# Expert stage of a graph and mixture-of-experts kernel: who issues the weight loads, and who copies the turned rows

## Chip, core and metric

The kernel runs on one core of one Trainium2 chip. The metric is the device time of one execution in microseconds (us), lower is better. The core has TensorE (PE in the views), VectorE (DVE), ScalarE (ACT), GpSimd (POOL) and SyncE (SP), each with its own stream of instructions that is carried out in order, and 16 DMA engines that they share. "SPq" or "ACTq" in a row is an instruction of that engine's queue that issues a DMA or waits.

## The reference, cut to what matters

The program is two graph layers and two mixture-of-experts layers on 10,000 rows of 512 numbers. The change touches only the last part of the second mixture layer: each row is sent to two of 64 experts, and each expert is a small net of two layers, 512 to 32 and 32 to 512, with a gelu between.

```python
se = sel.reshape(-1)                                   # 2 experts for each of the rows
pos = jnp.take_along_axis(jnp.cumsum(oh, axis=0) - 1, se[:, None], axis=1)[:, 0]
keep = pos < C
buf = jnp.zeros((E, C, d), x.dtype).at[se, posc].add(xr)
h = jax.nn.gelu(jnp.einsum('ecd,edf->ecf', buf, W1), approximate=False)   # W1: 64 x 512 x 32
y = jnp.einsum('ecf,efd->ecd', h, W2)                                     # W2: 64 x 32 x 512
out = y[se, posc] * keep[:, None].astype(x.dtype)
```

## The kernel before, in words

The kernel is a row of stages that follow each other with a barrier between; all but one stay as they are. The stage of the change ("the expert stage") computes `h` and `y` for the rows in the order of their experts. The 20,000 row copies, each expert's share rounded up to whole tiles of 128 rows, make 219 tiles (`LISTED`); a tile has one expert, and which one is read at run time from a small table `trow`. Tiles are worked in groups of four (`tiles(g)`, `NG` = 55 groups, the last has three). For a tile `t` of group `g`:

- **gather**: POOL fetches the tile's 128 rows with an indirect DMA into `xg`, a ring of eight tiles; it waits for the turn of tile `t - 8`.
- **weights**: SP reads the expert's number from `trow` (`value_load`) and issues two DMAs of 64 KB, the first layer's weights into `we1` and the second layer's into `we2`. Both are rings of `WR` = 6 groups, and both are counted on one semaphore per ring place, `p_w`. Before it starts a group, SP waits until the group six earlier is through its second layer (`p_dn`).
- **turn**: PE transposes the 128 x 512 tile in four matmuls into a PSUM bank; there are two banks for this, so it waits for the copy of tile `t - 2` (`p_T`).
- **copy**: ACT copies the turned tile from PSUM to `gT` (L2081).
- **up**: PE multiplies the four tiles of the group by `we1` (L2049), 16 matmuls in the program, each recorded as two.
- **gelu**: ACT writes `hg` from the result (L2089).
- **down**: PE multiplies `hg` by `we2`, one matmul for each tile into four PSUM banks (L2060), each recorded as two.
- **result**: DVE copies each of them from PSUM to `yo` (L2118), a ring of three groups; it waits for the store of the group three earlier (`p_st`).
- **store**: ACT issues one DMA of 1 MB from `yo` to memory for the group (L2094).

In round `g` of its loop PE does turns 1 and 2 of group `g`, `up(g - 1)`, turns 3 and 4 of `g`, `down(g - 2)`. ACT does two copies, `gelu(g - 1)`, two copies, `store(g - 3)`. The order on every engine is written out by hand, and nothing is reordered. The two waits on which PE's rounds hang are

```python
pe.wait_ge(p_T, tiles(g)[-1] + 1)       # up(g): the four turned tiles are copied
pe.wait_ge(p_w[g % WR], 32 * sum(len(tiles(k)) for k in range(g % WR, g + 1, WR)))  # both weights are there
```

Of the kernel before, what the change touches and what calls it, by code (L numbers as in the profile page):

```python
# [14 lines left out]
P = 128  # L15
# [47 lines left out]
def gnn_ffn(nc, x, xTt, src, dst, Wl, Wr, att, gbias, Wc0, b1c, W2e, b2e, WT, bG, hashp, M1, M2, out):  # L63
    ctx = ExitStack()
    with ctx:
# [1933 lines left out]
        we2 = sb("we2", [P, WR, D], F32, pt)  # L1999
        hg = sb("hg", [P, 2, P], F32, pt)  # L2000
        yo = sb("yo", [P, 12, D], F32, pt)
        p_ld, p_w, p_st = sems("p_ld", 8), sems("p_w", WR), sems("p_st", 3)
        p_0, p_tr, p_T, p_up, p_h, p_dn, p_y = (sem("p_" + n) for n in "0 tr T up h dn y".split())
        NG = -(-LISTED // 4)

# [4 lines left out]
        with nc.Block() as block:  # L2010
            @block.sync
            def _(sp):
                for g in range(NG):
                    if g >= WR:
                        sp.wait_ge(p_dn, tiles(g - WR)[-1] + 1)
                    for t in tiles(g):
                        e = sp.value_load(trow[0:1, t + 2 * P:t + 2 * P + 1], min_val=0, max_val=ME - 1)
                        j = t % 4
                        sp.dma_start(we1[:, g % WR, j, :], M1[bass.ds(e * P, P), :]).then_inc(p_w[g % WR], 16)
                        sp.dma_start(we2[MF * j:MF * (j + 1), g % WR, :], M2[bass.ds(e * MF, MF), :])\  # L2020
                            .then_inc(p_w[g % WR], 16)

            @block.gpsimd
            def _(pool):
# [9 lines left out]
            def _(pe):  # L2034
# [5 lines left out]

                def up(g):
                    pe.wait_ge(p_T, tiles(g)[-1] + 1)
                    pe.wait_ge(p_w[g % WR], 32 * sum(len(tiles(k)) for k in range(g % WR, g + 1, WR)))
                    if g >= 2:
                        pe.wait_ge(p_h, g - 1)
                    for k in range(DK):
# [6 lines left out]

                def down(g):
                    pe.wait_ge(p_h, g + 1)
                    for t in tiles(g):
                        j = t % 4
                        if g >= 1:
                            pe.wait_ge(p_y, t - 3)
                        nc.tensor.matmul(bank[4 + j], hg[MF * j:MF * (j + 1), g % 2, :],  # L2060
                                         we2[MF * j:MF * (j + 1), g % WR, :], start=True, stop=True).then_inc(p_dn, 1)
# [12 lines left out]

            @block.scalar
            def _(act):
                def copy(t):
                    act.wait_ge(p_tr, t + 1)
                    if t >= 8:
                        act.wait_ge(p_up, (t - 8) // 4 + 1)  # L2080
                    act.activation(gT[:, t % 8, :, :].rearrange("p k n -> p (k n)"), bank[t % 2], ACT.Copy)\  # L2081
                        .then_inc(p_T, 1)

                def gelu(g):
                    act.wait_ge(p_up, g + 1)
# [5 lines left out]
                def store(g):  # L2091
# [2 lines left out]
                    act.dma_start(YL[4 * g * P:(4 * g + n) * P, :].rearrange("(t p) c -> p t c", p=P),  # L2094
                                  yo[:, 4 * (g % 3):4 * (g % 3) + n, :]).then_inc(p_st[g % 3], 16)

                for g in range(NG + 3):
                    if g < NG:
                        for t in tiles(g)[:2]:
                            copy(t)  # L2100
                    if 1 <= g <= NG:
                        gelu(g - 1)
                    if g < NG:
                        for t in tiles(g)[2:]:
                            copy(t)
                    if g >= 3:
                        store(g - 3)
                for k in range(3):
                    act.wait_ge(p_st[k], 16 * len(range(k, NG, 3)))

            @block.vector
            def _(dve):
                for t in range(LISTED):
                    g = t // 4
                    if t % 4 == 0 and g >= 3:
                        dve.wait_ge(p_st[g % 3], 16 * (g // 3))
                    dve.wait_ge(p_dn, t + 1)
                    nc.vector.tensor_copy(yo[:, t % 12, :], bank[4 + t % 4]).then_inc(p_y, 1)  # L2118
        end_phase(pt)


# [135 lines left out]
```

## Time and profile before

| what | value |
|---|---|
| median of 3 runs | 3016.11 us (3004.85 to 3016.43) |
| the profiled execution, its own time | 3008.54 us |
| its span, first to last instruction | 3006.8 us |
| granted clock of TensorE, mean | 0.873 |
| first weight DMA issued / last result copied | 2282.9 us / 2753 us of the span |

The span is one execution; the time outside it is 1.74 us. A view that names a window counts from the start of the span. Busy time of an engine leaves out register, branch, semaphore and DMA-issuing instructions, so SP, which only issues, never shows as busy: how it spends its time is read from the starts of its rows. The DMA share is the mean busy share of the 16 DMA engines; as packets overlap it can pass 1.

### The profile page before, as it was taken

Reading aid. Unit: us, or ns where it says so; the run is one execution under the profiler, and the core shown is the slowest. Engines: PE = TensorE matmul, PEld = TensorE weight load, DVE = VectorE, ACT = ScalarE, POOL = GpSimd, SP = SyncE. Lnnn points to the kernel's source line nnn. Section 1 sums busy time; section 2 is a strip of 40 time slices with the busy share of each in tenths; the row PEclk is TensorE's granted clock in tenths of the full one; section 3 lists DMA queues with packets and bytes.
Section 4 is the critical chain, followed back from the end, with each engine's and each line's share of the span. In section 5 each row is a group of like instructions: output and inputs, shape, how many; then the busy total and the mean of one; then the engine's idle time right before and its main releaser. Section 6 shows DMA issues by size and latency. Waiting matters only on the chain. (4 is left out here: it accounts for less than half of the span.)

```text
span 3006.8 us, 43565 instructions
## 1 busy us (share of the span) xinstructions
PE 2155.7 (72%) x11422; PEld 1277.3 (42%) x11422; DVE 1674.5 (56%) x5206; ACT 1079.5 (36%) x2314; POOL 1992.6 (66%) x2711
## 2 busy tenths in 40 slices
PE   8999999677776577787867499999954656664000
PEld 3444444355554355455522156666632434442000
DVE  5666665455554787788711157777762222234665
ACT  0000000055553577777833245555532322231000
POOL 3677776677773688888866436777765444451776
PEclk9999999889998799999979799999976777786555
DMA  6999999389995666666489666676625888875999
GB/s 206 140 157 145 153 145 162 120 257 311 312 314 181 202 196 209 209 198 204 172 319 397 256 229 209 213 213 211 207 78 169 289 285 275 284 259 180 332 378 345
DMA packets 358165, 685.64 MB, mean 228 GB/s; under 512 B 54603, under 2 KB 88387, under 8 KB 357921
## 3 DMA queue, kind: packets, MB, share of 16 engines
q1 hardware_dynamic: 243096, 401.02, 47.5%
q0 software_dynamic: 80496, 218.00, 22.7%
q10 hardware_dynamic: 34329, 63.84, 6.2%
q8 instruction: 95, 1.56, 0.2%
q14 instruction: 149, 1.22, 0.1%
HBM read 433.75 MB, written 266.57 MB: 233 GB/s over the span
## 5 line engine op out<-in xcount | busy, mean ns | idle before, releaser
L2030 POOL DMA_INDIRECT xg<-n_rows,ids x219 | 218.4, 997 | 223.0 <-PE psum L155 177.9
L2118 DVE COPY yo<-psum 128x512 f32<-128x512 f32 x219 | 136.0, 684 | 335.7 <-PE psum L2060 335.7
L149 PE MATMUL psum<-wl,xT 128*128 128x512 f32 x632 | 288.8, 600 | 3.9 <-DVE xr L507 3.9
L149 PE MATMUL psum<-wg,yT 128*128 128x512 f32 x632 | 286.4, 596 | 0.0
L149 PE MATMUL psum<-wr,xT 128*128 128x512 f32 x632 | 284.1, 592 | 0.0
L149 PE MATMUL psum<-wc,x1T 128*128 128x264 f32 x632 | 174.7, 424 | 94.6 <-DVE hb L1165 93.5
L2167 POOL DMA_INDIRECT q<-slot_outputs,qs x158 | 171.9, 1088 | 95.7 <-issue 47.9
L1579 POOL DMA_INDIRECT slot_tokens<-sl x158 | 173.1, 1095 | 67.1 <-issue 51.2
L779 ACT ACT_TABLE_LOAD x1 | 1.3, 1283 | 588.4 <-PEq L80 588.4
L2049 PE MATMUL psum<-gT,we 128*32 128x128 f32 x1752 | 79.2, 336 | 164.8 <-issue 159.7
L149 PEld LDWEIGHTS psum<-wr,xT 128*128 128x128 f32 x632 | 120.1, 190 | 151.2 <-issue 151.2
L2081 ACT ACTIVATE gT<-psum 128x512 f32<-128x512 f32 x219 | 122.4, 595 | 166.3 <-PE psum L155 165.8
L149 PEld LDWEIGHTS psum<-wc,x1T 128*128 128x128 f32 x632 | 122.7, 204 | 128.6 <-issue 106.3
L1390 PE MATMUL psum<-gg,sm 128*128 128x512 f32 x236 | 129.0, 687 | 66.9 <-DVE sm L1378 57.1
L149 PEld LDWEIGHTS psum<-wl,xT 128*128 128x128 f32 x632 | 115.1, 190 | 125.9 <-issue 125.9
L149 PEld LDWEIGHTS psum<-wg,yT 128*128 128x128 f32 x632 | 114.7, 192 | 114.7 <-issue 114.7
L1369 POOL DMA_INDIRECT gg<-gcn_rows,idx x118 | 119.7, 1014 | 63.1 <-PE psum L1390 28.2
L650 POOL DMA_INDIRECT gl<-xl_rows,idx x118 | 134.6, 1141 | 39.5 <-issue 30.5
L654 POOL DMA_INDIRECT gr<-xr_rows,idx x118 | 133.7, 1133 | 36.0 <-issue 31.4
L155 PE MATMUL psum<-ident,xg 128*128 128x128 f32 x876 | 145.1, 317 | 16.5 <-DMA xg<-n_rows,ids 16.0
L149 PE MATMUL psum<-hp,x3T 128*128 128x256 f32 x632 | 150.0, 380 | 2.3 <-ACT x3T L1882 2.3
L1248 PE MATMUL psum<-w,hT 128*128 128x512 f32 x316 | 150.7, 600 | 0.0
(318 smaller groups left out, 5523.9 us busy)
## 6 DMA issues: line engine op xcount, KB each, us to landing
slot_outputs<-yo ACTq DMA_DIRECT2D x54, 1024.0 KB
x_rows<-x SPq DMA_DIRECT2D x158, 256.0 KB, 3.2
edge_sums<-eo SPq DMA_DIRECT2D x29, 1056.0 KB, 7.6
edge_sums<-go SPq DMA_DIRECT2D x29, 1024.0 KB
we<-in_M SPq DMA_DIRECT2D x438, 64.0 KB
xT<-in_xTt SPq DMA_DIRECT2D x79, 256.0 KB
xl_rows<-xl SPq DMA_DIRECT2D x79, 256.0 KB
xr_rows<-xr SPq DMA_DIRECT2D x79, 256.0 KB
```

The costliest lines, as they stand in the source:

```text
L149: last = nc.tensor.matmul(ps, lhs[:, k, :], rhs[:, k, :], start=(k == 0), stop=(k == DK - 1))
L155: last = nc.tensor.transpose(ps[:, k * P:(k + 1) * P], rows[:, k * P:(k + 1) * P], ident[:])
L650: pool.indirect_dma_start(gl[:, w % 16, :], None, XL, bass.IndirectOffsetOnAxis(idx[:, 0, w:w + 1], 0), bounds_check=NP - 1, oob_is_err=Fa ...
L654: pool.indirect_dma_start(gr[:, w % 8, :], None, XR, bass.IndirectOffsetOnAxis(idx[:, 1, w:w + 1], 0), bounds_check=NP - 1, oob_is_err=Fal ...
L1248: nc.tensor.matmul(bank[3 + 4 * h], hT[:, h, k, :], w2[:, k, :], start=(k == 0), stop=False)
L1369: pool.indirect_dma_start(gg[:, w % 8, :], None, GR, bass.IndirectOffsetOnAxis(idx[:, 0, w:w + 1], 0), bounds_check=NP - 1, oob_is_err=Fal ...
L1390: nc.tensor.matmul(bank[j], sm2[:, u % 2, j, :], gg[:, w % 8, :], start=True, stop=True)\
L1579: pool.indirect_dma_start(IDXF, bass.IndirectOffsetOnAxis(sl3[:, k, t:t + 1], 0), sl3[:, 2, t:t + 1], None, bounds_check=ME * SLOTS * P - ...
L2030: pool.indirect_dma_start(xg[:, t % 8, :], None, XN3, bass.IndirectOffsetOnAxis(ids[:, t:t + 1], 0), bounds_check=NP - 1, oob_is_err=False ...
L2081: act.activation(gT[:, t % 8, :, :].rearrange("p k n -> p (k n)"), bank[t % 2], ACT.Copy)\
L2118: nc.vector.tensor_copy(yo[:, t % 12, :], bank[4 + t % 4]).then_inc(p_y, 1)
L2167: pool.indirect_dma_start(q0[:, b % 3, t % 4, k, :], None, YL, bass.IndirectOffsetOnAxis(qs[:, b % 3, t % 4, k:k + 1], 0), bounds_check=LI ...
```

## The change

SP issues only the loads of the first layer's weights, and waits for `up` of the group six earlier in place of `down`. ACT issues the loads of the second layer's weights, three groups ahead of the group whose rows it is at, counted on semaphores of their own, `p_v`; `up` waits for `p_w` alone and `down` for `p_v`. The copies of the turned tiles move from ACT to DVE, which does the four copies of group `g` and then the four results of group `g - 2`. No DMA is added or taken away, and the bytes are the same.

```diff
-        p_ld, p_w, p_st = sems("p_ld", 8), sems("p_w", WR), sems("p_st", 3)
+        p_ld, p_w, p_v, p_st = sems("p_ld", 8), sems("p_w", WR), sems("p_v", WR), sems("p_st", 3)
...
             def _(sp):
                 for g in range(NG):
                     if g >= WR:
-                        sp.wait_ge(p_dn, tiles(g - WR)[-1] + 1)
+                        sp.wait_ge(p_up, g - WR + 1)
                     for t in tiles(g):
                         e = sp.value_load(trow[0:1, t + 2 * P:t + 2 * P + 1], min_val=0, max_val=ME - 1)
-                        j = t % 4
-                        sp.dma_start(we1[:, g % WR, j, :], M1[bass.ds(e * P, P), :]).then_inc(p_w[g % WR], 16)
-                        sp.dma_start(we2[MF * j:MF * (j + 1), g % WR, :], M2[bass.ds(e * MF, MF), :])\
-                            .then_inc(p_w[g % WR], 16)
+                        sp.dma_start(we1[:, g % WR, t % 4, :], M1[bass.ds(e * P, P), :]).then_inc(p_w[g % WR], 16)
...
                 def up(g):
-                    pe.wait_ge(p_w[g % WR], 32 * sum(len(tiles(k)) for k in range(g % WR, g + 1, WR)))
+                    pe.wait_ge(p_w[g % WR], 16 * sum(len(tiles(k)) for k in range(g % WR, g + 1, WR)))
...
                 def down(g):
                     pe.wait_ge(p_h, g + 1)
+                    pe.wait_ge(p_v[g % WR], 16 * sum(len(tiles(k)) for k in range(g % WR, g + 1, WR)))
...
             def _(act):
-                def copy(t):
-                    act.wait_ge(p_tr, t + 1)
-                    if t >= 8:
-                        act.wait_ge(p_up, (t - 8) // 4 + 1)
-                    act.activation(gT[:, t % 8, :, :].rearrange("p k n -> p (k n)"), bank[t % 2], ACT.Copy)\
-                        .then_inc(p_T, 1)
+                def weights(g):
+                    if g >= WR:
+                        act.wait_ge(p_dn, tiles(g - WR)[-1] + 1)
+                    for t in tiles(g):
+                        e = act.value_load(trow[0:1, t + 2 * P:t + 2 * P + 1], min_val=0, max_val=ME - 1)
+                        j = t % 4
+                        act.dma_start(we2[MF * j:MF * (j + 1), g % WR, :], M2[bass.ds(e * MF, MF), :])\
+                            .then_inc(p_v[g % WR], 16)
...
+                for g in range(3):
+                    weights(g)
                 for g in range(NG + 3):
-                    if g < NG:
-                        for t in tiles(g)[:2]:
-                            copy(t)
                     if 1 <= g <= NG:
                         gelu(g - 1)
-                    if g < NG:
-                        for t in tiles(g)[2:]:
-                            copy(t)
                     if g >= 3:
                         store(g - 3)
+                    if g + 3 < NG:
+                        weights(g + 3)
...
             def _(dve):
-                for t in range(LISTED):
+                def copy(t):
+                    dve.wait_ge(p_tr, t + 1)
+                    if t >= 8:
+                        dve.wait_ge(p_up, (t - 8) // 4 + 1)
+                    nc.vector.tensor_copy(gT[:, t % 8, :, :].rearrange("p k n -> p (k n)"), bank[t % 2]).then_inc(p_T, 1)
+
+                def result(t):
                     g = t // 4
                     if t % 4 == 0 and g >= 3:
                         dve.wait_ge(p_st[g % 3], 16 * (g // 3))
                     dve.wait_ge(p_dn, t + 1)
                     nc.vector.tensor_copy(yo[:, t % 12, :], bank[4 + t % 4]).then_inc(p_y, 1)
+
+                for g in range(NG + 2):
+                    for t in tiles(g) if g < NG else ():
+                        copy(t)
+                    for t in tiles(g - 2) if g >= 2 else ():
+                        result(t)
```

On SP, one tile in the middle of the stage stood so before (the load of the expert's number, two register instructions, the weights of each layer with a register instruction ahead of each):

```order
L2017 TENSOR_LOAD trow
L2017 ISA x2
L2019 ISA
L2019 DMA we<-in_M 128x128
L2020 ISA
L2020 DMA we<-in_M 32x512
```

The same place after the change:

```order
L2017 TENSOR_LOAD trow
L2017 ISA x2
L2018 ISA
L2018 DMA we<-in_M 128x128
L2017 TENSOR_LOAD trow
```

The second DMA and its register instruction are gone from SP's tile, and the next tile's number follows at once.

On ACT, one round in the middle of the stage stood so before (copies to `gT`, the gelu to `hg`, the store from `yo`; the semaphores have the allocator's names):

```order
L2089 ACTIVATE hg<-psum 128x128 [waits a_xr,a_mm]
L2081 ACTIVATE gT<-psum 128x512 [waits a_mm,a_nm] x2
L2094 DMA slot_outputs<-yo 128x4x512 [waits a_m]
L2081 ACTIVATE gT<-psum 128x512 [waits a_mm,a_nm] x2
L2089 ACTIVATE hg<-psum 128x128 [waits a_xr,a_mm]
```

And now, from the gelu through the store to the first two of the four weight loads that follow it:

```order
L2089 ACTIVATE hg<-psum 128x128 [waits a_nq,a_al]
L2094 DMA slot_outputs<-yo 128x4x512 [waits a_aw]
L2079 TENSOR_LOAD trow [waits a_nq]
L2079 ISA x2
L2081 ISA
L2081 DMA we<-in_M 32x512
L2079 TENSOR_LOAD trow
L2079 ISA x2
L2081 ISA
L2081 DMA we<-in_M 32x512
```

The four copies are gone from ACT's round, and four loads of a number with one DMA each stand behind the store, ahead of the next gelu.

## Rows read from the trace of the kernel before

**Rows 1.** Busy time by stretch of the expert stage.

```profile
...
core 0: us, PE busy (x) PEld busy (x) DVE busy (x) ACT busy (x) POOL busy (x), PEclk, DMA share, GB/s
2283.00:2313.00 30.00, 18.40 (x183) 12.67 (x184) 3.22 (x6) 11.47 (x21) 23.13 (x22) 0.74 0.75 218
2313.00:2743.00 430.00, 264.13 (x2847) 180.08 (x2845) 127.16 (x205) 127.07 (x254) 197.74 (x199) 0.80 0.84 274
2743.00:2758.00 15.00, 6.17 (x38) 2.90 (x38) 5.60 (x10) 0.27 (x1) 0.00 (x0) 0.61 0.59 215
...
```

**Rows 2.** Who waited for whom, 2282 to 2775 us: total, times, longest.

```profile
...
DVE yo L2118 <- PE psum L2060: 335.7, 54, 24.8
...
POOL xg L2030 <- PE psum L155: 177.9, 77, 9.9
PEld psum L2049 <- issue: 171.1, 51, 10.2
...
PEld psum L155 <- DMA xg<-n_rows,ids: 21.6, 14, 9.4
...
PEld psum L2049 <- ACT gT L2081: 5.7, 4, 1.8
...
```

**Rows 3.** Users of the weight tiles up to 2528.2 us: ns min/median/max, first and last start.

```profile
...
L2049 PE MATMUL psum<-gT,we x896: 269/297/423, 2298.0 to 2522.5; 128*32 128x128 f32 x180
...
L2019 SPq DMA_DIRECT2D we<-in_M x116: 337/348/1273, 2282.9 to 2527.2; - x116
...
L2020 SPq DMA_DIRECT2D we<-in_M x116: 331/332/1508, 2283.5 to 2527.7; - x116
...
```

**Rows 4.** Timeline ahead of the `up` at 2533 us.

```profile
...
2523.85 0.37 ACTq L2094 DMA_DIRECT2D slot_outputs<-yo  x1
...
2524.17 1.51 SPq L2020 DMA_DIRECT2D we<-in_M  x1
...
2527.16 0.35 SPq L2019 DMA_DIRECT2D we<-in_M  x1
...
2527.69 0.33 SPq L2020 DMA_DIRECT2D we<-in_M  x1
...
2528.87 0.35 SPq L2019 DMA_DIRECT2D we<-in_M  x1
...
2530.51 0.35 SPq L2019 DMA_DIRECT2D we<-in_M  x1
...
2533.25 1.08 PE L2049 MATMUL psum<-gT,we 128*32 128x128 f32 x16 [7.36 <-issue]
```

**Rows 5.** Both weight DMAs of SP and `up`, whole stage.

```profile
...
L2049 PE MATMUL psum<-gT,we x1752: 269/273/423, 2298.0 to 2746.3; 128*32 128x128 f32 x195
...
L2019 SPq DMA_DIRECT2D we<-in_M x219: 337/348/1273, 2282.9 to 2740.2; - x110
...
L2020 SPq DMA_DIRECT2D we<-in_M x219: 331/332/1749, 2283.5 to 2740.7; - x110
...
```

**Rows 6.** POOL's timeline, gathers that wait for nothing.

```profile
...
2287.53 1.00 POOL L2030 DMA_INDIRECT xg<-n_rows,ids  x1 [0.30 <-issue]
2288.83 1.00 POOL L2030 DMA_INDIRECT xg<-n_rows,ids  x1 [0.31 <-issue]
...
```

**Rows 7.** Costliest groups by form, 2282 to 2775 us.

```profile
...
L2118 DVE COPY yo<-psum 128x512 f32<-128x512 f32 x219 | 136.0, 684 | 335.7 <-PE psum L2060 335.7
L2081 ACT ACTIVATE gT<-psum 128x512 f32<-128x512 f32 x219 | 122.4, 595 | 166.3 <-PE psum L155 165.8 <-issue 0.3
...
L2089 ACT ACTIVATE hg<-psum 128x128 f32<-128x128 f32 x54 | 15.0, 278 | 203.2 <-PE psum L2049 203.2
...
```

**Rows 8.** Timeline of PE, DVE and ACT, a round at either clock.

```profile
...
2500.49 1.14 PE L2060 MATMUL psum<-we,hg 32*128 32x512 f32 x8
...
2501.56 1.09 PE L155 MATMUL psum<-ident,xg 128*128 128x128 f32 x8
...
2501.72 2.48 DVE L2118 COPY yo<-psum 128x512 f32<-128x512 f32 x4 [7.92 <-PE psum L2060]
...
2502.26 1.08 ACT L2081 ACTIVATE gT<-psum 128x512 f32<-128x512 f32 x2 [1.02 <-PE psum L155]
...
2502.59 1.08 PE L2049 MATMUL psum<-gT,we 128*32 128x128 f32 x32
...
2504.62 1.14 PE L2060 MATMUL psum<-we,hg 32*128 32x512 f32 x8
...
2505.69 1.09 PE L155 MATMUL psum<-ident,xg 128*128 128x128 f32 x8
...
2515.01 1.94 PE L2049 MATMUL psum<-gT,we 128*32 128x128 f32 x32 [8.23 <-issue]
...
2516.88 1.97 PE L155 MATMUL psum<-ident,xg 128*128 128x128 f32 x8
...
2518.78 1.96 PE L2060 MATMUL psum<-we,hg 32*128 32x512 f32 x8
...
```

**Rows 9.** DMA queues and issues, 2282 to 2775 us: packets, MB, share.

```profile
...
q10 hardware_dynamic: 28912, 57.41, 33.2%
q0 software_dynamic: 17520, 41.01, 25.5%
q1 hardware_dynamic: 43104, 30.83, 21.9%
...
qx<-x_rows SPq DMA_DIRECT2D x2, 1024.0 KB, 7.8
...
```

**Rows 10.** Windows in which the DMA engines are full.

```profile
...
2315.00:2320.00 5.00, 2.27 (x16) 1.15 (x16) 0.79 (x2) 1.10 (x2) 3.86 (x4) 1.00 1.02 339
2320.00:2325.00 5.00, 3.42 (x42) 2.71 (x41) 1.70 (x3) 1.47 (x3) 4.00 (x4) 0.75 1.05 354
2325.00:2330.00 5.00, 3.17 (x22) 1.86 (x20) 2.48 (x4) 2.28 (x4) 3.08 (x4) 0.91 1.01 342
2330.00:2335.00 5.00, 3.70 (x48) 2.56 (x48) 0.00 (x0) 1.47 (x3) 1.90 (x2) 0.77 1.01 346
...
```

**Rows 11.** The last stage, full too.

```profile
...
2845.00:2920.00 75.00, 0.00 (x0) 0.00 (x0) 50.72 (x81) 0.00 (x0) 58.53 (x55) 0.50 1.01 371
...
```

## The prediction

> **What bounds the kernel now.** I take the stage first. The windows show that it lasts some 470 us and that no engine is busy all the time: in the long middle stretch PE is busy 264 of 430 us, DVE 127, ACT 127, POOL 198, and the DMA share is 0.84 at 274 GB/s [rows 1]. So the stage waits for something that is not busy time. The table of waits names it by exclusion: DVE and POOL wait for PE (335.7 and 177.9 us), and PE in turn waits 171.1 us ahead of `up` for "issue", which is the name for a wait whose releaser the view doesn't know; for gathers it waits 21.6 us, for ACT's copies 5.7 us [rows 2]. `up` waits for copies, for the gelu of two groups before and for the weights, and the weights are the one of these that the view can't name.
>
> Counting confirms it. Up to 2528.2 us SP had issued 116 loads of each kind, which is 29 groups, while PE had 896 records of `up`, 28 groups of 32 [rows 3]. The last DMA of group 29 went out at 2527.69, and its `up` starts at 2533.25 after 7.36 us of idle time [rows 4]. The ring would let SP be six groups ahead; it is never more than one. So SP's stream sets the pace: from the first `up` at 2298.0 to the last, whose records end the row at 2746.3 and which starts some 1.5 us ahead of that, 54 rounds take 446.8 us, **8.27 us a round** [rows 5].
>
> Where does SP's time go? When nothing disturbs it, tile follows tile every 1.64 us (2528.87 to 2530.51 [rows 4]), though its two DMA instructions take only 0.348 and 0.332 us [rows 5]; the rest is reading the number and preparing registers. 219 tiles at 1.64 us are 359 us. From first to last issue it is 457.8 us [rows 5], so 99 us, 1.8 us a round, are extra. They come in bursts behind a store: ACT issues one at 2523.85, and SP's DMA at 2524.17 takes 1.51 us instead of 0.33, the next starts 3.0 us later [rows 4].
>
> **The change, part by part.** I work out the pace that each resource would allow in a round of four tiles; the slowest sets it.
>
> *SP.* A tile loses the step from its first DMA to its second, 0.53 to 0.54 us (2527.16 to 2527.69 [rows 4]): 1.64 − 0.54 = 1.10, 4.4 us a round undisturbed. With all of the extra 1.8 us it is 6.2. The new wait for `up` six groups back stands ahead of loads that are then several groups early; it costs nothing while SP is ahead.
>
> *ACT.* It loses four copies of 0.56 us [rows 7]. It gains four loads, each a number read and one DMA. No row shows ACT doing this; the nearest are SP's, so 1.1 us each, 4.4 in all. With the store's 0.37 [rows 4] and the gelu's 0.28 [rows 7] that is 5.1 us. If ACT takes the extra 1.8 us too, 6.9. Behind the loads on ACT stand the next gelu and store; the gelu is needed by a `down` one round later, so up to a round's delay is covered. The twelve loads ahead of the loop take 13 us; PE's first `up` comes 15 us after SP's first issue [rows 5], so they are covered too, with about 2 us to spare.
>
> *DVE and PE.* DVE gains 219 copies of the form that it already does in 0.684 us [rows 7], four in a row in 2.48 us [rows 8]: eight copies are some 5.0 to 5.5 us. They are chained to PE. At the high clock (2.4 GHz) the first result starts 1.23 us after `down` (2500.49 to 2501.72), four results end 2.5 us later, then the copy of the next group's first tile follows, 0.6 to 0.7 us and 0.3 for the release. Only then can PE do the third turn; two turns (0.55 us each, 1.09 for both [rows 8]) and the next `down` follow. That is 1.23 + 2.5 + 0.9 + 1.1 = **5.75 us** a round. PE's own work is 4.13 us (2501.56 to 2505.69). At the low clock (1.2 GHz) turns take 1.97 a pair, `up` 1.94, `down` 1.96, so PE's work alone is 7.84 us [rows 8].
>
> *POOL.* 1.30 us a gather (2287.53 to 2288.83 [rows 6]), 5.2 us a round.
>
> *DMA.* The three queues moved 57.41 + 41.01 + 30.83 = 129.25 MB, of which 2.1 MB (the two `qx` loads) belong to the next stage [rows 9]: 127.2 MB, 2.31 MB a round. What do the engines give when full? In four windows in a row the share is at or above 1.01 at 339 to 354 GB/s [rows 10], mean 345. That is **6.7 us a round**; at 354 it is 6.5. Now they run at 274 GB/s [rows 1].
>
> The slowest is the DMA, before every engine's stream. The bursts behind the stores fit this: they fall where the engines are full. I take 7.1 us, 6% above the floor, since gathers come in pairs behind the turns and PE falls to the low clock in some waits. Start-up (2283 to 2298) and tail (after the last `up`) stay. The sum: 54 × (8.27 − 7.1) = 63 us off 3008.5 us, the profiled execution's own time, 2945.3. That execution lies 7.6 us under the median and 3.7 above the lowest run; half way between the two, at 3012.3, I start from: **2949 us**, 2.2% less than the median.
>
> Two rules of the Trainium skill bear on this. "DMA: Bandwidth & Descriptors", section "Issuing engines are not separate DMA queues", says that to start DMAs on several engines only saves sequencer time, usually small beside the transfer. By that rule the change would be worth little; the trace shows that here the sequencer's time is what is late. The same page puts HBM for a core at about 358 GB/s, by which a round would be 6.5 us and the time some 13 us less than with 6.7; the last stage shows 371 GB/s [rows 11], so it is not a hard ceiling in this kernel, and with this stage's mix of small loads no window passed 354.
>
> **The rivals.**
>
> *A, the forecast (0.68):* DMA-bound, 6.6 to 7.6 us a round, 36 to 90 us gained.
>
> *B, the extra time behind the stores moves to both queues (0.22).* What lengthens SP's DMA instructions might be not full engines but the generation of the store's descriptors, which both queues share. For it: the delay begins within 0.3 us of the store's issue [rows 4]. Against it: it lasts longer than the store's own 0.37 us. ACT now issues its first load right behind its own store and SP's loads compete too. If ACT gets one and a half times the present extra, a round is 5.1 + 2.7 = 7.8 us, and the gain 25 us: 2987 us on the same scale. At 5.1 + 3.2 nothing is gained. The skill's "Perfetto Trace Analysis", section "DMA Instruction — HWDGE (DVE, Sync)", describes such a shared block with a lock; this trace can't tell it from full engines.
>
> *C, no gain (0.05).* PE stays at the low clock, which alone makes 7.84 us a round, and the waits for gathers bring it above 8. Against it: PE at the low clock with 7.84 of work a round would be busy throughout, and the round that followed a wait of 8.23 us ran at the low clock while one without a wait ran at the high one [rows 8]. Within 15 us of before.
>
> *D, slower (0.05): the copies wait behind the results.* On DVE a result of group `g` waits until the store of group `g − 3` has landed. Before, only results stood behind it; now the turned tiles' copies do, and with them PE. The store has about three rounds less four results to be issued and to land: 3 × 7.1 − 2.5 = 18.8 us. ACT may issue it up to 5 us late. A 1 MB transfer takes 7.8 us from issue to landing in the next stage [rows 9], and 1.04 MB at a third of 345 GB/s would take 9.1 us, so 14 us or less is used. It decides when issue and landing together pass 3 × 8.27 − 2.5 = 22.3 us; then each 3 us more cost 1 us a round. With 27 us a round would be 9.8 us, 83 us slower, 3095 us.
>
> **How the numbers follow.** Three runs of this kernel differ by 0.4%; about 0.5%, 15 us, is what can be told from no change. A lies between 2922 and 2976, B between 2976 and 3004. The bounds of the floor (6.5 at 354 GB/s, gain 96 us) give 2916 at the low end; 7.84 us a round gives a gain of 23 us and 2989 at the high end. The range of **2916 to 2989** leaves out about 2 in 10: part of B, and C and D. Faster by over 0.5% (under 3001): nearly all of A and B, 0.88. Within 0.5%: the rest of B, and C, 0.07. Slower: 0.05.
>
> **What the profile after would show.** Right: the DMA share of the middle stretch at 0.93 or more and 315 to 340 GB/s; the first to last `up` in 365 to 400 us; PE's "issue" wait ahead of `up` gone or under 40 us, since SP is several groups ahead; PE waiting for gathers more than 21.6 us. Copies on DVE at 0.68 us. B would show itself by ACT's DMA and SP's lasting long with a share under 0.9, and by `down` or the gelus late. D: DVE idle ahead of `yo`, and POOL waiting for PE longer than 178 us. I would be wrong if loads cost ACT much more than the 1.1 us of SP, or if the full engines move this mix at under 300 GB/s.

## The result and the profile after

The kernel after takes 2914.15 us (median, 2910.81 to 2920.22 in 4 runs) against 3010.48 us before; the ratio is 0.9677, 95% interval 0.9647 to 0.9707, so it is 3.2% faster. The prediction said 2949 us and a range of 2916 to 2989: right way, but the time lies 2 us below the range. The profiled execution took 2912.88 us against 3008.54, 95.7 us less where 63 was worked out.

The windows of the stretches after, which answer to [rows 1]; the middle stretch is cut where the tiles become empty (columns as there):

```profile
...
core 0: us, PE busy (x) PEld busy (x) DVE busy (x) ACT busy (x) POOL busy (x), PEclk, DMA share, GB/s
2288.00:2318.00 30.00, 19.22 (x176) 12.80 (x176) 13.21 (x20) 2.12 (x4) 23.12 (x22) 0.68 0.89 249
2318.00:2600.00 282.00, 204.56 (x2340) 130.82 (x2336) 207.12 (x333) 11.65 (x42) 167.74 (x169) 0.90 1.05 366
2600.00:2650.00 50.00, 38.98 (x504) 25.38 (x504) 44.22 (x73) 2.22 (x8) 29.89 (x30) 1.00 0.81 263
...
```

The DMA share of the long stretch went from 0.84 at 274 GB/s to 1.05 at 366 GB/s, and DVE's busy time from 30% to 73%. From 2600 us on the share falls to 0.81, since those tiles hold hardly any rows: in that window the gather queue moves 0.26 MB. The DMA view of it (queue: packets, MB, share):

```profile
...
q10 hardware_dynamic: 6236, 11.49, 66.4%
q1 hardware_dynamic: 2822, 1.28, 9.3%
q0 software_dynamic: 2570, 0.26, 4.2%
...
```

The users of the weight tiles, which answer to [rows 5] (ns min/median/max, first and last start):

```profile
...
L2046 PE MATMUL psum<-gT,we x1752: 272/273/423, 2303.8 to 2653.7; 128*32 128x128 f32 x195
...
L2081 ACTq DMA_DIRECT2D we<-in_M x219: 327/328/3992, 2287.8 to 2638.8; - x110
L2018 SPq DMA_DIRECT2D we<-in_M x219: 337/338/1912, 2287.8 to 2625.5; - x110
...
```

First `up` to last `up` took 447 us and takes 349, **6.47 us a round** in place of 8.27. SP ends its loads 27 us ahead of the last `up`, in place of 4. ACT's load instruction reaches 3992 ns: the delays that SP alone had, ACT has now too. The waits in the stage answer to [rows 2]:

```profile
...
PE psum L155 <- DVE gT L2115: 87.7, 50, 4.9
POOL xg L2027 <- PE psum L155: 86.3, 70, 4.8
...
DVE yo L2122 <- DMA slot_outputs<-yo: 43.7, 19, 4.0
...
PEld psum L155 <- DMA xg<-n_rows,ids: 19.9, 14, 9.4
...
PEld psum L2046 <- issue: 9.9, 54, 0.3
...
```

PE's wait ahead of `up` for a releaser that the view can't name fell from 171.1 to 9.9 us. New are 87.7 us in which PE's third turn waits for DVE's copy, and 43.7 us in which DVE waits for a store to land. Two rounds of the last stretch, PE and DVE, which answer to [rows 8]:

```profile
...
2619.84 1.09 PE L155 MATMUL psum<-ident,xg 128*128 128x128 f32 x8
2619.99 2.49 DVE L2122 COPY yo<-psum 128x512 f32<-128x512 f32 x4 [0.42 <-PE psum L2058]
...
2620.86 1.08 PE L2046 MATMUL psum<-gT,we 128*32 128x128 f32 x32
...
2622.39 1.28 DVE L2115 COPY gT<-psum 128x512 f32<-128x512 f32 x2
...
2623.22 1.23 PE L155 MATMUL psum<-ident,xg 128*128 128x128 f32 x8 [1.28 <-DVE gT L2115]
...
2623.89 1.29 DVE L2115 COPY gT<-psum 128x512 f32<-128x512 f32 x2 [0.21 <-PE psum L155]
...
2624.38 1.14 PE L2058 MATMUL psum<-we,hg 32*128 32x512 f32 x8
...
2625.45 1.09 PE L155 MATMUL psum<-ident,xg 128*128 128x128 f32 x8
...
2631.06 1.09 PE L155 MATMUL psum<-ident,xg 128*128 128x128 f32 x8
...
```

The first turn starts at 2619.84, 2625.45 and 2631.06: **5.61 us a round**, the chain that the prediction put at 5.75. In it the third turn waits 1.28 us for the first copy (2623.22), and DVE is busy all but 0.6 us. The stretch before is a mix of such rounds and longer ones: by the starts of `up`, 22 of the first 45 rounds take less than 5.75 us and the others up to 11.7, so their mean of 6.67 us is a pace over many rounds, and not the length of a typical one.

### The profile page after: what moved, and what is told of

The parts are those of the page before. It is cut to its first block and busy times, and to the rows that moved or that the text cites. A ratio compares the mean times of both kernels' runs of the same rounds, so it can differ in the third digit from the quotient of the medians.

```text
span 2911.1 us, 44199 instructions
## 1 busy us (share of the span) xinstructions
PE 2142.8 (74%) x11396; PEld 1260.6 (43%) x11422; DVE 1812.3 (62%) x5425; ACT 957.5 (33%) x2095; POOL 1991.2 (68%) x2711
## 5 line engine op out<-in xcount | busy, mean ns | idle before, releaser
L155 PE MATMUL psum<-ident,xg 128*128 128x128 f32 x876 | 143.2, 304 | 102.6 <-DVE gT L2115 87.7
L155 PEld LDWEIGHTS psum<-ident,xg 128*128 128x128 f32 x876 | 105.7, 154 | 176.7 <-issue 156.8
L2122 DVE COPY yo<-psum 128x512 f32<-128x512 f32 x219 | 135.9, 684 | 65.8 <-DMA slot_outputs<-yo 43.7
L2115 DVE COPY gT<-psum 128x512 f32<-128x512 f32 x219 | 142.1, 685 | 34.0 <-PE psum L155 33.8
L393 POOL DMA_INDIRECT node_rows<-qv,idx x118 | 121.8, 1032 | 46.3 <-issue 41.3
```

What stands on the lines that cost most here:

```text
L155: last = nc.tensor.transpose(ps[:, k * P:(k + 1) * P], rows[:, k * P:(k + 1) * P], ident[:])
L393: pool.indirect_dma_start(NQF, bass.IndirectOffsetOnAxis(idx[:, 2, w:w + 1], 0), qv[:, w:w + 1], None, bounds_check=NP - 1, oob_is_err=False)\
L2115: nc.vector.tensor_copy(gT[:, t % 8, :, :].rearrange("p k n -> p (k n)"), bank[t % 2]).then_inc(p_T, 1)
```

## The experiments

The runs were made on more than one chip, and fell in two groups: in one the kernel before takes 3007 to 3010 us, in the other 3091 to 3104 (called chips of the slower kind). Ratios compare runs of one chip; where times of a stage from two kinds of chip stand beside each other, it is said. What makes the two groups is open: chip number 0 of the record stands in both (3007 and 3098 us). "First to last `up`" is read from the row of the matmuls into `psum` from `gT` and `we`, less the 1 to 1.5 us that the last group's records take.

**Was SP's stream the limit before?** Three edits, all on a chip of the slower kind; on that kind the whole change gives about as much as on the first (3010.41 against 3104.42 us, 3.0%, one execution each). The first keeps the split of the loads but leaves the copies on ACT (against the kernel after):

```diff
             def _(act):
+                def copy(t):
+                    act.wait_ge(p_tr, t + 1)
...
                 for g in range(NG + 3):
+                    if g < NG:
+                        for t in tiles(g)[:2]:
+                            copy(t)
...
             def _(dve):
-                for g in range(NG + 2):
-                    for t in tiles(g) if g < NG else ():
-                        copy(t)
```

> The kernel after, but the copies of the turned tiles stay on ScalarE, two ahead of the gelu and two behind it; VectorE does results only. Theory 1 (before, SyncE's stream of instructions set the pace; the split is what gains): SyncE is several groups ahead of up and its wait is gone. ScalarE's round is then the longest: four copies 2.2 to 2.4 us, gelu 0.28, store 0.37, four loads of about 1.25 us each as in the kernel after, some 8 us, in one stream, so most of the gain is lost: 2975 to 3010 us. Rival (SyncE's stream was not the limit, ScalarE's copies were, and moving them gave the gain): slower than before by the 4 x 1.1 us a round that ScalarE gains, 54 x 4.4 = 240 us at most.

Measured: ratio 0.9956 (0.9937 to 0.9975), 439.5 us from first to last `up`. Its timeline (start, length) shows why:

```profile
...
2602.51 0.28 ACT L2096 ACTIVATE hg<-psum 128x128 f32<-128x128 f32 x1
...
2603.41 0.60 ACT L2079 ACTIVATE gT<-psum 128x512 f32<-128x512 f32 x1 [0.61 <-PE psum L155]
...
2604.26 0.60 ACT L2079 ACTIVATE gT<-psum 128x512 f32<-128x512 f32 x1 [0.26 <-PE psum L155]
2604.27 0.39 ACTq L2101 DMA_DIRECT2D slot_outputs<-yo  x1
2605.39 5.55 ACTq L2088 DMA_DIRECT2D we<-in_M  x4
...
2611.04 1.09 ACT L2079 ACTIVATE gT<-psum 128x512 f32<-128x512 f32 x2 [6.18 <-DMA slot_tokens<-sl]
...
2611.78 0.41 PE L155 MATMUL psum<-ident,xg 128*128 128x128 f32 x2 [3.77 <-ACT gT L2079]
```

ACT issues the four loads from 2605.39 to 2610.94, and only then copies; PE's third turn waits 3.77 us for it. The split alone gives 0.4%.

The second moves the copies to DVE and leaves SP both loads (against the kernel before):

```diff
             def _(act):
-                    if g < NG:
-                        for t in tiles(g)[:2]:
-                            copy(t)
...
             def _(dve):
-                for t in range(LISTED):
+                for g in range(NG + 2):
+                    for t in tiles(g) if g < NG else ():
+                        copy(t)
+                    for t in tiles(g - 2) if g >= 2 else ():
+                        result(t)
```

> The kernel before, but VectorE copies the turned tiles (four copies, then four results, as in the kernel after); SyncE still issues both layers' weights. Theory 1 (SyncE's stream is the limit): the pace stays at 8.3 us a round, within 15 us of before (3000 to 3025), up still waits for weights. Rival (the copies' move gains by itself): 30 us or more faster.

Measured: ratio 1.0006 (0.9986 to 1.0026). The move of the copies alone gives nothing. The third doubles the suspected cost (against the kernel before):

```diff
                     for t in tiles(g):
-                        e = sp.value_load(trow[0:1, t + 2 * P:t + 2 * P + 1], min_val=0, max_val=ME - 1)
+                        for _ in range(2):
+                            e = sp.value_load(trow[0:1, t + 2 * P:t + 2 * P + 1], min_val=0, max_val=ME - 1)
```

> The kernel before, but SyncE reads each tile's expert number twice; nothing is added for DMA or the other engines. A number read and its register steps take about 0.57 us of SyncE (tile to tile 1.64 us with 0.35 + 0.19 + 0.33 us for the two DMAs and the rest for the number). Theory 1: the whole 219 x 0.57 = 125 us shows less what the stalls behind stores give back: 60 to 125 us slower, 3070 to 3135. Rival (full DMA engines or the round of PE set the pace, SyncE's instructions do not): under 15 us slower.

Measured: ratio 1.040 (1.036 to 1.044), 119 us between the medians; the rows of the tile `we`:

```profile
...
L2050 PE MATMUL psum<-gT,we x1752: 269/421/423, 2380.4 to 2952.8; 128*32 128x128 f32 x195
...
L2020 SPq DMA_DIRECT2D we<-in_M x219: 2/343/697, 2365.9 to 2948.1; - x110
...
L2021 SPq DMA_DIRECT2D we<-in_M x219: 3/332/1568, 2366.5 to 2948.6; - x110
...
```

SP's loads last 582.7 us, and 219 tiles at 1.64 + 0.57 are 484, which leaves 99 us of extra, as in the kernel before. Of the 219 × 0.57 = 125 us that SP was given, 119 showed in the time. So SP's stream was the limit, and the gain needs both parts of the change: the split frees SP, and the move frees ACT to take the loads.

**What holds the kernel after?** Five candidates: the landing latency of stores with a ring of three groups, the chain of DVE and PE, ACT's stream, full DMA engines, and descriptor making. The ring of results at five groups (against the kernel after, all places of it alike):

```diff
-        yo = sb("yo", [P, 12, D], F32, pt)
+        yo = sb("yo", [P, 20, D], F32, pt)
...
-                    if t % 4 == 0 and g >= 3:
-                        dve.wait_ge(p_st[g % 3], 16 * (g // 3))
+                    if t % 4 == 0 and g >= 5:
+                        dve.wait_ge(p_st[g % 5], 16 * (g // 5))
```

> The kernel after, with the ring of results at five groups in place of three. In the kernel after VectorE waits 43.7 us in 19 waits for stores to land. Theory 2 (the 16 DMA engines are full, so landing is late because of throughput): the waits for stores go, but the time moves to gathers or weights; within 10 us of the kernel after (2905 to 2925). Rival (the wait is a matter of latency and ring length): VectorE's wait goes and the pace comes near the 5.6 us of undisturbed rounds: 54 x (6.45 - 5.6) = 46 us less at most, 2870 to 2885.

Measured: ratio 0.9755 (0.9717 to 0.9794) on a chip of the slower kind, where no kernel after stood beside it, so this run alone decides nothing. It was repeated with the kernel after on one chip:

> The kernel after, unchanged, as the measure for the other runs on this chip: 0.968 of the kernel before, as measured (0.965 to 0.971).

> The kernel after with five groups in the ring of results, on the same chip as the kernel after. Theory 2 (full DMA engines): the ratio to before within 0.003 of that of the kernel after. Rival (landing latency and ring length): 0.010 to 0.015 lower.

Measured: 0.9681 (0.9633 to 0.9729) and 0.9667 (0.9619 to 0.9716), 2915.12 and 2911.65 us. DVE's wait for stores, 45.8 us in this run of the kernel after, is gone with five groups; the time is not:

```profile
...
DVE yo L2122 <- PE psum L2058: 64.9, 54, 5.2
PE psum L155 <- DVE gT L2115: 53.5, 46, 1.6
...
PEld psum L2058 <- ACT hg L2089: 42.2, 33, 4.0
...
```

DVE now waits 64.9 us for PE, where it waited 18.2 in the kernel after beside it, and `down` waits 42.2 us for ACT's gelu, where it waited 0.5. The waits moved to other engines. From first to last `up` this profile has 344.4 us against 351.9, but the 30 to 45 us of the rival did not come: latency was not the limit.

The chain of DVE and PE, with three quarters of each copy left out (against the kernel after):

```diff
+                nc.vector.memset(gT[:], 0.0).then_inc(p_z, 1)
+                dve.wait_ge(p_z, 1)
...
-                    nc.vector.tensor_copy(gT[:, t % 8, :, :].rearrange("p k n -> p (k n)"), bank[t % 2]).then_inc(p_T, 1)
+                    nc.vector.tensor_copy(gT[:, t % 8, 0, :], bank[t % 2][:, 0:P]).then_inc(p_T, 1)
```

> The kernel after, but VectorE copies only the first 128 of a turned tile's 512 columns (the rest of the buffer is set to zero once), so three quarters of the first layer's sum are left out; all DMAs stay. VectorE's round falls by about 4 x 0.4 = 1.6 us and the chain of VectorE and PE from 5.6 to some 4.2 us. Theory 2 (the 16 DMA engines are full): the pace of the rounds that fetch whole tiles does not move, about 6.4 us or more (2.44 MB at 380 GB/s); only the last rounds, whose tiles are empty, get faster: 0 to 20 us less than the kernel after, and ScalarE's loads at about 5.1 us a round take over there. Rival (the chain of VectorE and PE sets the pace, with single late stores on top): 40 us or more less.

Measured: 2906.0 us, ratio 0.9660 (0.9615 to 0.9704) beside the 0.9677 and 0.9681 of the kernel after, 344.3 us from first to last `up`. A window of it:

```profile
...
2400.00:2500.00 100.00, 68.19 (x832) 45.18 (x824) 51.98 (x120) 4.17 (x15) 58.47 (x60) 0.91 1.04 361
...
```

DVE is busy 52 of 100 us where it was 73, and PE records as much work as in the kernel after (832 records against 833). By the starts of `up` the first 45 rounds take 6.68 us on the mean, where they took 6.67, and only the last nine fell, from 5.43 to 4.85. The chain was not the limit in full rounds.

ACT's stream, with two of the four second-layer loads given to SP and a ring of five (against the kernel after, beside the ring's lines):

```diff
-                        sp.wait_ge(p_up, g - WR + 1)
+                        sp.wait_ge(p_dn, tiles(g - WR)[-1] + 1)
...
+                        if j >= 2:
+                            sp.dma_start(we2[MF * j:MF * (j + 1), g % WR, :], M2[bass.ds(e * MF, MF), :])\
+                                .then_inc(p_v[g % WR], 16)
...
-                    for t in tiles(g):
+                    for t in tiles(g)[:2]:
                         e = act.value_load(trow[0:1, t + 2 * P:t + 2 * P + 1], min_val=0, max_val=ME - 1)
```

> The kernel after with five groups in the ring of results, and SyncE also loads the second layer's weights of the third and fourth tile of a group, so that ScalarE loads only two; the same bytes. Theory 2: no faster than the ring alone in full rounds, within 0.003 of the ratio of the kernel after. If ScalarE's stream limits after the ring is longer: 10 to 20 us less than with the ring alone.

Measured: 0.9684 (0.9639 to 0.9730), no faster. `down` no longer waits for the gelu; in its place stands:

```profile
...
PEld psum L2050 <- issue: 42.8, 42, 4.3
...
```

This is `up` waiting for what the view can't name, 10.2 us with the ring alone, and SP ends its loads only 3 us ahead of the last `up`. So the run took load off ACT but brought SP's stream near the limit again, and does not clear ACT's stream by itself.

Then bytes. First without the second layer's weights after the sixth group (against the kernel after):

```diff
-                    pe.wait_ge(p_v[g % WR], 16 * sum(len(tiles(k)) for k in range(g % WR, g + 1, WR)))
+                    pe.wait_ge(p_v[g % WR], 64)
...
-                    if g + 3 < NG:
+                    if g + 3 < WR:
                         weights(g + 3)
```

> The kernel after, but the second layer's weights are loaded for the first six groups only and used again for all later ones: 12.8 of 127 MB and nearly all of ScalarE's loads are left out, all gathers stay. Theory 2 (full engines, 363 GB/s in full rounds): a full round moves 2.18 MB, 6.0 us in place of 6.7, the rounds of empty tiles stay at 5.6: some 30 us less than the kernel after. If ScalarE's stream (about 6.1 us a round) were the limit instead: the same 5.6 us in all rounds and no wait for stores, 45 us less. If neither is (a store takes its time whatever else moves): within 10 us.

Measured: 2874.17 us, ratio 0.9559 (0.9519 to 0.9600), 41 us less than the kernel after on the same chip. A window of it:

```profile
...
2400.00:2500.00 100.00, 73.80 (x943) 49.06 (x932) 83.80 (x135) 4.72 (x17) 67.08 (x68) 0.98 1.03 368
...
```

A round has 56 records of PE; 943 in 100 us are 16.8 rounds, 5.94 us each where 6.0 was expected. At 368 GB/s and 2.18 MB a round that is the rate of the kernel after, which speaks for the bytes; and from first to last `up` it takes 313.9 us in place of 351.9, 38 less, where 12.8 MB at 366 GB/s are 35. The time of the execution alone would not: 41 us less lies nearer to the 45 expected if ACT's stream were the limit than to the 30 of full engines, and DVE's wait for stores is nearly gone (2.2 us). What tells the two apart is the next run, in which ACT keeps all of its loads.

Then with half of the gathers (against the kernel after):

```diff
                 for t in range(LISTED):
+                    if t >= 8 and t % 2:
+                        continue
...
-                    pe.wait_ge(p_ld[t % 8], 16 * (t // 8 + 1))
+                    pe.wait_ge(p_ld[t % 8], 16 if t % 2 else 16 * (t // 8 + 1))
```

> The kernel after, but after the first eight tiles only every second tile is gathered; the others work on rows fetched earlier. This leaves out half the gathered bytes, about 20 MB of 127, and half of GpSimd's instructions. Theory 2 (full engines): a round moves 2.0 MB, 5.3 to 5.5 us at 360 to 380 GB/s, under the 5.6 us of the chain of VectorE and PE, so the waits for stores nearly vanish: 54 x (6.45 - 5.7) = 40 us less than the kernel after, near 2875. Rival (the stores land late for a reason of their own, such as the generation of their descriptors, or the loads behind them in ScalarE's queue): VectorE's wait for stores stays near 40 us and the time within 15 us of the kernel after.

Measured: 2886.92 us, ratio 0.9597 (0.9555 to 0.9640), 320.6 us from first to last `up`; the waits for stores are gone. The first 45 rounds fell from 6.67 to 5.97 us on the mean with ACT's loads as they were, so ACT's stream was not what held them at 6.67. The gain is smaller than the bytes alone would give: 100 us in the middle hold 16 rounds of 6.25 us. Its timeline shows what comes next:

```profile
...
2426.57 0.28 ACT L2091 ACTIVATE hg<-psum 128x128 f32<-128x128 f32 x1 [5.71 <-issue]
2426.59 0.39 ACTq L2096 DMA_DIRECT2D slot_outputs<-yo  x1
...
2426.90 1.14 PE L2060 MATMUL psum<-we,hg 32*128 32x512 f32 x8 [0.27 <-ACT hg L2091]
...
2428.03 4.59 ACTq L2083 DMA_DIRECT2D we<-in_M  x4
...
2432.72 0.28 ACT L2091 ACTIVATE hg<-psum 128x128 f32<-128x128 f32 x1 [5.88 <-issue]
2432.75 0.39 ACTq L2096 DMA_DIRECT2D slot_outputs<-yo  x1
...
2433.06 1.14 PE L2060 MATMUL psum<-we,hg 32*128 32x512 f32 x8 [0.48 <-ACT hg L2091]
...
```

From gelu to gelu ACT takes 6.15 us, with four loads between, and `down` waits 0.27 and 0.48 us for it. In such rounds ACT's stream sets the pace: the 5.1 us worked out plus 1.0 us of delay, 0.5 us less than the 6.67 of the kernel after.

**Where SP's extra 99 us came from.** The kernel before with half of the gathers (the same edit):

> The kernel before, but after the first eight tiles only every second tile is gathered; half of the gathered bytes are left out. SyncE's stream shows 99 us above the undisturbed 1.64 us a tile. If full DMA engines lengthen it, the extra shrinks with the load: at 107 MB in place of 127 a round of 7 us needs only 290 GB/s, the extra falls by half or more and the time by 40 to 60 us. If the store's own descriptors lengthen it (a block that both queues share), the extra stays at 80 to 99 us and the time within 20 us of before.

Measured: ratio 0.9988 (0.9968 to 1.0008); SP's loads last 461.0 us against 464.1 in the run with the copies alone moved, on the same kind of chip. The extra stayed with 20 MB less to move and the DMA share down at 0.72 (2400 to 2800 us), against what the prediction said of it. Next, the same bytes in a quarter of the descriptors (against the kernel before; the last stage turns the row numbers to match):

```diff
-                    act.dma_start(YL[4 * g * P:(4 * g + n) * P, :].rearrange("(t p) c -> p t c", p=P),
+                    n = 4
+                    act.dma_start(YL[4 * g * P:(4 * g + n) * P, :].rearrange("(p t) c -> p t c", t=4),
```

> The kernel before, but a store writes each partition's four result rows next to each other in memory (runs of 8 KB in place of 2 KB, same bytes, a quarter of the runs), and the last stage works out the moved row numbers (six more small VectorE instructions a block). Theory 3 (SyncE's extra 99 us come from making the store's descriptors, which SyncE's own DMAs wait for): the extra falls with the number of runs to 25 to 50 us and the pace to some 7.2 to 7.6 us a round: 35 to 60 us faster. Rival (the extra comes from moving the bytes): the extra stays near 99 us, the time within 10 us of before.

Measured: ratio 1.0017 (0.9999 to 1.0035). The packets of ACT's queue fell from 28912 [rows 9] to 7920 at the same bytes, and SP's loads last 458.8 us as before. The theory of descriptor making falls. The DMA view of this run:

```profile
...
q10 hardware_dynamic: 7920, 57.68, 31.6%
q0 software_dynamic: 17552, 41.07, 26.9%
q1 hardware_dynamic: 42048, 28.73, 21.1%
...
```

The same edit on the kernel after, and with the ring of five:

> The kernel after with the same longer runs. Theory 2 (full engines set the pace in full rounds): two packets of 2 KB took 0.084 us each by the median and one of 4 KB 0.159, so stores cost 5% less, 0.1 to 0.2 us a round: 5 to 10 us less than the kernel after, a ratio to before of 0.962 to 0.967. If making descriptors held the kernel after back: 20 us less or more.

> The kernel after with longer runs and five groups in the ring of results: the sum of both, 8 to 14 us less than the kernel after, a ratio to before of about 0.964 by theory 2. Clearly below that only if the waits for stores were latency.

Measured: 0.9704 (0.9671 to 0.9738) and 0.9727 (0.9687 to 0.9767), no gain, if anything a loss; 5 to 10 and 8 to 14 us less were expected. The last stage has more small instructions in these runs, but the loss is not only there: first to last `up` take 352.9 and 353.9 us. Last, half of the stored bytes (against the kernel before; the last stage reads another tensor, so only the expert stage is compared):

```diff
-                    n = len(tiles(g))
+                    n = min(2, len(tiles(g)))
```

> The kernel before, but a store writes only the first two tiles of its group (half of the stored bytes, 28 MB, are left out), and the last stage gathers from another tensor, so only the expert stage's times are compared. If SyncE's extra goes with the bytes that a store moves, it halves: from 96 us to about 50, and first to last up from 447 to 400 to 415 us. If it comes once for each store whatever its size, it stays at 85 to 100 us and the pace at 8.2 to 8.3 us a round.

Measured, in one execution on a chip of the slower kind: 410.6 us from first to last `up`, 7.60 us a round. The rows of the loads:

```profile
...
L2019 SPq DMA_DIRECT2D we<-in_M x219: 2/348/697, 2378.1 to 2800.4; - x110
...
L2020 SPq DMA_DIRECT2D we<-in_M x219: 2/332/1290, 2378.7 to 2800.9; - x110
...
```

SP's loads last 422.8 us, 64 above 359, where the run with the copies alone moved has 105. In both, 10 us of this come ahead of the first store and have another cause. Half of the bytes took away 41 us, so if the rest follows in proportion, an estimate, the bytes of the stores account for 82 of the 105; fewer descriptors and fewer gathers had changed nothing. The expected 50 was too low. That SP stands while the burst of 1 MB fills the queues of the engines is an inference; these runs don't show the queues.

**Half the stores in the kernel after**, the counterpart of the last:

> The kernel after with the same half stores. Theory 2: a full round moves 1.92 MB, 5.3 us at 363 GB/s, less than the 5.6 us of the chain of VectorE and PE: 5.6 to 5.8 us in every round, first to last up 305 to 313 us in place of 349. If ScalarE's loads (about 6.1 us a round with its gelu and store) hold it, as they did with half the gathers: 325 us or more.

Measured, in one execution: 367.7 us, far from 305 to 313, on a chip of the slower kind. With the kernel after beside it on such a chip:

> The kernel after, unchanged, as the measure for the next run on the same chip. Where before takes about 3010 us: first to last up 349 to 352 us. Where before takes about 3095 us, as on the chip of the last two runs: some 365 us, since there PE also halts within its matmul groups.

> The kernel after with half of the stored bytes left out, compared with the kernel after of the same chip by the time from first to last up. If full DMA engines hold the kernel after: 36 to 45 us less (5.6 to 5.8 us a round on a chip with before at 3010). If something else does: within 10 us.

Measured, in one execution each: 371.7 and 369.2 us. A window of the kernel after:

```profile
...
2480.00:2580.00 100.00, 78.31 (x818) 47.11 (x820) 73.33 (x117) 3.89 (x14) 59.05 (x60) 0.93 1.05 364
...
```

The same window with half stores:

```profile
...
2480.00:2580.00 100.00, 77.10 (x792) 47.10 (x791) 69.11 (x112) 3.88 (x14) 56.65 (x57) 0.91 0.89 274
...
```

The rate fell from 364 to 274 GB/s and the pace stayed. So on this kind of chip the engines' bytes are not the limit, though the share stood at 1.05 as on the first kind: the share alone does not show what sets the pace. The counterpart on the first kind was not run; there the two runs above with fewer bytes stand for it. The timeline of PE in the kernel after on it:

```profile
...
2507.50 1.09 PE L155 MATMUL psum<-ident,xg 128*128 128x128 f32 x8
2508.53 1.34 PE L2046 MATMUL psum<-gT,we 128*32 128x128 f32 x24
2510.95 0.52 PE L2046 MATMUL psum<-gT,we 128*32 128x128 f32 x8 [1.08 <-issue]
2511.85 1.23 PE L155 MATMUL psum<-ident,xg 128*128 128x128 f32 x8 [0.39 <-DVE gT L2115]
...
2514.08 1.09 PE L155 MATMUL psum<-ident,xg 128*128 128x128 f32 x8
...
```

An `up` of 32 records, 1.08 us elsewhere, stands still for 1.08 us after 24 of them, with no wait in the program at that place; the round is 6.58 us (2507.50 to 2514.08), about the 5.6 us of the chain and one halt. Counted in the trace, there are 44 gaps of over 0.3 us inside the groups of `up` in this run, 24.5 us together, and none in the kernel after on the first kind of chip, where first to last `up` take 22.5 us less. Their cause stays open.

No version beat the kernel after clearly; the ring of five is 3.5 us lower with overlapping intervals.

## Why the prediction was wrong in size, point by point

- *SP's stream bounds the kernel before.* Right: 119 us more when SP reads its number twice, and the wait ahead of `up` went from 171.1 to 9.9 us.
- *SP and ACT after.* Right as far as it mattered: SP is ahead, and ACT's round is 6.15 us in the run with half of the gathers, where 5.1 to 6.9 was given. It is not the limit, but only 0.5 us behind it.
- *The chain of DVE and PE at 5.75.* Measured 5.61.
- *The floor of the DMA engines and the 6% above it.* This is the step that failed, "I take 7.1 us, 6% above the floor". The mechanism was right, and both sizes in the term were not. The rate: 345 GB/s came from 20 us near the stage's start, when the engines showed a share of 1.01 to 1.05; in the kernel after they hold 366 GB/s at 1.05 for 282 us, by which the prediction's 2.31 MB a round take 6.32 us and not 6.7: 54 × 0.38 = 20.5 us. The surcharge: 0.4 us were added on grounds that no row measured; the measured 6.47 lies 0.15 us above 6.32, or 2.4%: 54 × 0.25 = 13.5 us. Together they are the 34 us between 63 and 97. As rounds are not even, this splits an average and is not a measurement of each part.
- *An even round.* The bytes are not even. The first 45 rounds take 6.67 us and the last nine 5.4, because the last tiles are almost empty; a full round moves 2.44 MB and not 2.31. In the average the two cancel, but what limits differs: DMA first, the chain last. The prediction had the same floor in every round.
- *The bursts fall where the engines are full.* Wrong as argued: the extra stays with half of the gathers and a share of 0.72. Rival B's premise, that it would move to both queues, came true in part (ACT's 1.0 us a round), its cause (descriptors) did not, and the slower pace of the DMA hid it. The section that the prediction named for it ("Perfetto Trace Analysis", "DMA Instruction — HWDGE (DVE, Sync)", of the Trainium skill) names VectorE and SyncE as the engines that share the block, not ScalarE, and no run here shows the block.
- *Rival D, copies behind the results.* It came in a small form: DVE waits for stores 43.7 us. The longer ring shows that this cost next to nothing: 3.5 us between the medians, with overlapping intervals.
- *The rule on issuing engines* ("DMA: Bandwidth & Descriptors", section "Issuing engines are not separate DMA queues", of the Trainium skill), by which the gain would be only sequencer time: it was only that, and it was worth 3.2%, because the sequencer was what was late.
- *The low end.* 54 × (8.27 − 6.5) = 96 us was the bound from the best single window of 5 us; the kernel passed it over the whole stage, with 97. A best window seen while another engine starves the DMA is no upper bound. That the time fell just outside the range is a close call: it started from 3012.3 us, and 3010.48 were measured, which is nearly all of the 2 us.
- *The signs.* The nameless wait ahead of `up` is under 40 us as said (9.9). The share is over 0.93, but the 366 GB/s and the 349 us lie outside 315 to 340 and 365 to 400, by the same failed step. PE's wait for gathers did not grow: 19.9 us, where more than 21.6 was said.

## What to carry to other kernels

An engine whose views show no busy time can set the pace: count what a DMA-issuing engine has issued against what its user has used, and time issue to issue. When the limit moves to the DMA engines, read their rate from stretches in which they are full for long, and add a surcharge only with a row behind it: here, with rings several groups deep, 2.4% was left where 6% was added. Don't take a high DMA share as proof that bytes set the pace; leave bytes out and look. Freeing one engine's stream and loading another's can be one change: here either half alone gave 0.4% and nothing.

## What the runs showed of the hardware that was not expected

- A 1 MB store from one queue goes with 1.8 us more in the other queue's stream, whatever the number of its descriptors (28912 or 7920 packets) and with half of the gathered bytes beside it; with half of the store's bytes it is 1.2 us (64 us over 55 stores).
- A DMA share over 1 doesn't mean one rate: it was 1.05 at 366 GB/s in the kernel after and 1.03 at 328 GB/s with half of the gathers. There each packet took longer: by the traces 198 ns in place of 180 on the mean for 4 KB, and 96 in place of 88 for 2 KB. Why is open.
- Runs in memory of 8 KB in place of 2 KB for the stores did not shorten the stage: 352.9 us from first to last `up`, against 349.2 and 351.9 in two profiles of the kernel after.
- Runs of the kernel before fall in two groups 3% apart, and in the slower one PE halts for about 1.1 us inside matmul groups in which the program has no wait.
